# A two-layer attention and mixture-of-experts kernel: three routing batches, expert weights prepared early and kept in DRAM, 8 of 32 shared tiles moved behind the routed ones

## The reference, cut to what matters

```python
x = x + L0_ffn(L0_cond(x))        # attention with 16 heads; relu^2 FFN of 1024, then a 5-step spike count
x = x + L1_ffn(L1_cond(x))        # attention with 16 heads; then the block below

def L1_ffn(X):
    nx = rmsnorm(X, g1)
    X = X + attention4(nx)                          # 4 heads, one shared K and V
    xf = rmsnorm(X, g2)
    rw = softmax(xf @ Wr.T + expert_bias)           # 8 experts
    topw, topi = top_k(rw, 2); topw = softmax(topw)
    shared = swiglu(xf, sW1, sW2, sW3)              # every token
    eo[e] = (silu(xf @ eW1[e].T) * (xf @ eW3[e].T)) @ eW2[e].T
    return X + shared + sum over the 2 chosen e of topw * eo[e]
```

## Time and profile before

| | us |
|---|---|
| runs (3) | 1443.48, 1443.55, 1451.34; median 1443.55 |
| the profiled execution, its own time | 1444.31 |
| its span, first to last instruction | 1442.6 |
| mean granted TensorE clock | 0.962 of full speed |

### The profile page before, as it was taken

One profiled execution on the slowest core, in us unless ns is written; L12 is line 12 of the kernel. 1 busy time (PEld: TensorE's weight loads), 2 busy tenths in 40 slices (PEclk: granted clock), 3 DMA queues, 4 the chain that ended last, 5 costly groups with the idle time before them and its releaser, 6 DMA issues.

```text
span 1442.6 us, 43140 instructions
## 1 busy us (share of the span) xinstructions
PE 1299.9 (90%) x15310; PEld 1147.9 (80%) x15311; DVE 1035.3 (72%) x2129; ACT 896.2 (62%) x2309; POOL 710.8 (49%) x797
## 2 busy tenths in 40 slices
PE   4899999999689999889999999689998689999990
PEld 4799999998579999778888888568877578888870
DVE  4798988888736555787887787778887576555546
ACT  3676777767356666656666676477776254555545
POOL 2556565564435454445445444367766662333330
PEclk9899999999799999999999999899999899999995
DMA  8200000001030000000000000020001623333319
GB/s 230 54 9 10 8 11 8 8 10 38 2 87 1 1 0 1 3 10 10 9 8 10 9 8 13 21 58 15 16 15 63 221 87 116 104 104 101 103 42 349
DMA packets 87021, 71.15 MB, mean 49 GB/s; under 512 B 49981, under 2 KB 80831, under 8 KB 85824
## 3 DMA queue, kind: packets, MB, share of 16 engines
q1 hardware_dynamic: 80320, 51.73, 12.6%
q0 software_dynamic: 6528, 17.05, 3.3%
HBM read 39.47 MB, written 24.02 MB: 44 GB/s over the span
## 4 chain that ended last, share of the span: by engine, by line
PE 53%; issue 21%; POOL 10%; DVE 9%; ACT 4%; another core or an unknown queue 1%; DMA 1%; DVEq 0%; ACTq 0%; POOLq 0%; SPq 0%
PE psQ L2332 8%; PE psQ L1946 7%; PE psW L2024 7%; PE psW L2311 5%; POOL pn L758 5%; PE psQ L2137 3%; POOL rq L784 3%; PE psS L2137 3%; PE psW L2125 3%; PE psM L2125 3%; PE psS L2048 2%; PE psT L1975 2%; PE psT L2059 2%; PE psM L1998 2%; PE psT L2319 2%
## 5 line engine op out<-in xcount | busy, mean ns | idle before, releaser
L1946 PE MATMUL psQ<-xT,wq 128*128 128x256 f32 x1536 | 225.2, 298 | 3.5 <-ACT cur L1114 1.8
L1946 PEld LDWEIGHTS psQ<-xT,wq 128*128 128x128 f32 x1536 | 205.3, 201 | 4.5 <-issue 2.5
L2024 PE MATMUL psW<-wout,oT 128*128 128x256 f32 x1536 | 205.5, 292 | 1.1 <-ACT oT L977 1.1
L2024 PEld LDWEIGHTS psW<-wout,oT 128*128 128x128 f32 x1536 | 194.3, 197 | 1.3 <-ACT oT L977 1.3
L2332 PE MATMUL psQ<-W,exT 128*128 (+1 forms) x624 | 171.2, 410 | 0.0
L758 POOL TENSOR_TENSOR pn<-ex,rden 128x1024 f32<-128x1024 f32 x64 | 124.5, 1945 | 43.5 <-DVE rden L1437 43.5
L977 ACT ACTIVATE oT<-psT,small 128x512 fp32r<-128x512 f32 x128 | 81.1, 685 | 91.3 <-PE psT L2059 91.2
L802 POOL TENSOR_TENSOR hT<-hf,hT 128x512 fp32r<-128x512 f32 x64 | 85.9, 1341 | 102.1 <-ACT hT L1110 101.9
L912 POOL DMA_INDIRECT results<-result,idx x72 | 70.1, 974 | 133.7 <-ACT result L1241 128.7
L770 POOL TENSOR_TENSOR masked_bias<-bias_t,negmask 128x1024 f32<-128x1024 f32 x32 | 68.9, 2152 | 132.5 <-DVE ex L1405 132.5
L1364 DVE SCALAR_TENSOR_TENSOR oT<-psT,small,oT 128x512 fp32r<-128x512 f32 x128 | 90.2, 746 | 55.9 <-ACT oT L977 55.9
(11 more groups left out here) (302 smaller groups left out, 3374.6 us busy)
## 6 DMA issues: line engine op xcount, KB each, us to landing
rows<-sorted SPq DMA_DIRECT2D x72, 132.0 KB, 2.1
both<-results SPq DMA_DIRECT2D x8, 1024.0 KB, 11.8
raw_w<-W SPq DMA_DIRECT2D x27, 256.0 KB, 3.8
vv<-vp SPq DMA_DIRECT2D x256, 16.0 KB, 1.8
out<-X SPq DMA_DIRECT2D x8, 512.0 KB, 8.8
X<-x SPq DMA_DIRECT2D x1, 3584.0 KB, 18.4
bvv<-v_all SPq DMA_DIRECT2D x128, 16.0 KB, 1.8
sorted<-rows SPq DMA_DIRECT2D x9, 132.0 KB
```

Of the source, the lines that this page charges most:

```text
L1946: mm = nc.tensor.matmul(psQ[:, cc, h * QT:h * QT + QT], wq[w][:, k, c * P:c * P + P], xT[g % 2][u][:, k, :], start=(k == 0 and j == 0), st ...
L2024: mm = nc.tensor.matmul(psW[:, 0:D], oT[u][:, c, :], wout[w][:, c, :], start=(u == 0 and c == 0 and w == 0), stop=(u == 1 and c == CH - 1))
```

## The change: what it does

1. **Weights.** A new pass lies in the FFN. SP loads pieces of 256 KB of raw weights into four buffers (two in the place of `xT`, two in `ffn_work`), DVE alone makes hi and lo (`split_piece`), SP writes both (512 KB) to a DRAM array `parked`, waits until that has landed, and only then loads piece n+4. The 27 pieces lie between the FFN groups on DVE, by `PARKED`. `load_expert` becomes one DMA of 1.5 MB per expert from `parked`; the second expert's is issued once the first has landed. `split_expert` goes.
2. **Routing** has three batches of 12, 12 and 8. The first two are ranked inside the block; 14 of the 64 sends lie in block steps 26 to 39, one a step; the later ones are gated by `(t - 7) * 22 // 24 + 1` transposed tiles.
3. **Order.** `FIRST` is 24: 24 shared tiles, 72 routed, 8 shared.
4. **Weights of the tokens** are worked out in shared steps 9 to 21, with ACT's exponentials in steps 18 and 20.
5. **The end.** ACT and DVE do part of the scaling and summing between steps 103 and 107; groups 1, 3 and 5 are added by GpSimd.
6. DVE's and GpSimd's block loops, and DVE's FFN loop, are written out.

```diff
-FIRST = TILES
+FIRST = 3 * TILES // 4
-BATCHES = ((0, 20), (20, TILES))
-FIRST_CHOICE, SECOND_CHOICE, RANK, PLACES = (-6, 5), (-5, 6), (-2, 7), (-1, 8)
-SENT_AHEAD = 3
-ENDS, SLOTS, MARGINS = (10, 12, 14), (16, 18, 20, 22, 24), 26
+BATCHES = ((0, 12), (12, 24), (24, TILES))
+FIRST_CHOICE, SECOND_CHOICE, PLACES = (-14, -2, 5), (-13, -1, 6), (-11, 1, 8)
+RANKED_BEFORE, RANK = (19, 31), 7
+SEND_STEP, SENT_IN_BLOCK = 26, 14
+ENDS, SLOTS, WEIGHTS = (10, 11, 12), (13, 14, 15, 16, 17), (9, 18, 20, 22)
+POOL_GROUPS = (1, 3, 5)
+SCALE_STEP, SUM_STEP = {103: 0, 104: 1, 105: 2, 106: 3, 107: 4}, {104: 0, 106: 2}
+PARKED = [4, 5, 5, 5, 4, 4, 0]
+PIECES = KD + 1
 # SP, behind the loads of layer 1
+            def park(n):
+                p, part = divmod(n, PIECES)
+                sp.wait_ge(sem("p_lo"), n + 1)
+                sp.dma_start(parked[p, :, :, part * 2 * D:part * 2 * D + 2 * D], piece[n % 4][:].bitcast(F32)).then_inc(sem("p_kept"), 16)
+                sp.wait_ge(sem("p_kept"), 16 * (n + 1))
+            for n in range(4):
+                load_piece(n)
+            for n in range(PIECES * EP):
+                park(n)
+                if n + 4 < PIECES * EP:
+                    load_piece(n + 4)
             def load_expert(p, slot, done):
-                w13 = raw_w[:, slot, 1, 0:2 * KD * D].rearrange("p (k w n) -> p k w n", k=KD, w=2)
...
+                sp.dma_start(W[:, slot, :, :].bitcast(F32), parked[p]).then_inc(done, 16)
             sp.wait_ge(sem("t_oev"), 2 * TILES)
-            for p in range(2):
-                load_expert(p, SHARED_SLOT + p, sem("e_first"))
+            load_expert(0, SHARED_SLOT, sem("e_weights"))
+            sp.wait_ge(sem("e_weights"), 16)
+            load_expert(1, SHARED_SLOT + 1, sem("e_weights"))
...
-            for p in (3, EP - 1, EP - 2):
-                load_expert(p, (p + 1) % EP, sem("e_rest"))
-            for p in range(4, EP - 2):
-                load_expert(p, p + 1, sem("e_last"))
+            for p in range(3, EP):
+                load_expert(p, (p + 1) % EP, sem("e_weights"))
 # GpSimd
+                if n >= SENT_IN_BLOCK and k == 0:
+                    pool.wait_ge(sem("e_xTp"), (t - SENT_IN_BLOCK // TOP_K) * 22 // 24 + 1)
+                send(t, k)
...
+            for n, g in enumerate(POOL_GROUPS):
+                x = X[:, G4 * g:G4 * g + G4, :]
+                pool.wait_ge(sem("y_scaled"), g + 1)
+                nc.gpsimd.tensor_tensor(x, x, both[g][:, :, 0, :], ALU.add).then_inc(sem("y_half"), 1)
+                pool.wait_ge(sem("y_half"), 2 * n + 1)
+                nc.gpsimd.tensor_tensor(x, x, both[g][:, :, 1, :], ALU.add).then_inc(sem("y_half"), 1)
 # ACT
             def first_half(i):
-                for piece in range(3 * EP):
-                    if SPLIT_STEP[piece] == i:
-                        split_expert(piece // 3, piece % 3)
+                if i == WEIGHTS[1]:
+                    act.wait_ge(sem("r_exp_in"), 2)
+                    nc.scalar.activation(logits[:], logits[:], ACT.Exp).then_inc(sem("r_exp"), 1)
+                    nc.scalar.activation(top_w[1][:], top_w[1][:], ACT.Exp).then_inc(sem("r_exp"), 1)
+                elif i == WEIGHTS[2]:
+                    act.wait_ge(sem("r_exp_in"), 3)
+                    nc.scalar.activation(weight[1], weight[1], ACT.Exp).then_inc(sem("r_exp"), 1)
...
-                for k in ((0, 1) if g % 2 else (1,)):
+                for k in ((0, 1) if g in POOL_GROUPS else (1,)):
...
+            def other_half(i):
+                if i in SCALE_STEP:
+                    if i == min(SCALE_STEP):
+                        act.wait_ge(sem("r_exp_in"), 4)
+                    scale_results(SCALE_STEP[i])
 # DVE
+            def split_piece(n):
+                part = n % PIECES
+                hi, lo = piece[n % 4][:, 0, :], piece[n % 4][:, 1, :]
+                raw = raw_piece[n % 4][:, 1, :]
+                dve.wait_ge(sem(f"p_raw{n % 4}"), ...)
+                if part < KD:
+                    then(nc.vector.tensor_scalar(hi, raw, g2col[:, part:part + 1], None, ALU.mult))
+                    ins = nc.vector.scalar_tensor_tensor(lo, raw, g2col[:, part:part + 1], hi.bitcast(F32), ALU.mult, ALU.subtract)
+                else:
+                    then(nc.vector.tensor_copy(hi, raw))
+                    ins = nc.vector.tensor_tensor(lo, raw, hi.bitcast(F32), ALU.subtract)
+                ins.then_inc(sem("p_lo"), 1)
...
+            for g in range(GROUPS):
+                ffn(g, g % 2, first=g == 0, last=g == GROUPS - 1)
+                if g < GROUPS - 1:
+                    for n in range(sum(PARKED[:g]), sum(PARKED[:g + 1])):
+                        split_piece(n)
+                if g == 0:
+                    dve.wait_ge(sem("t_oev"), TILES)
```

More of the change, by code:

```diff
@@ L158, in pipeline, with expert_steps @@
             between(i)
-SPLIT_STEP = [-4, -3, -2, 0, 1, 2, 3, 4, 5] + list(range(10, 28))
-def expert_steps(eng, step, first_half=None):
+PARKED = [4, 5, 5, 5, 4, 4, 0]
+PIECES = KD + 1
+assert sum(PARKED) == PIECES * EP
+def expert_steps(eng, step, first_half=None, other_half=None):
     end = FIRST + ROUTED
@@ L505, in rank_columns @@
             n = BATCHES[b][1] - BATCHES[b][0]
[L506 removed]
+            return psM[:, 0:(n + 1) * E] if b == 2 else psW[:, D:D + (n + 1) * E]
         def rank_bank(b):
@@ L676, in _ @@
             for g in range(GROUPS):
-                sp.wait_ge(sem("y_acc"), g + 1)
+                done = sum(h not in POOL_GROUPS for h in range(g + 1))
+                if g in POOL_GROUPS:
+                    sp.wait_ge(sem("y_half"), 2 * (g + 1 - done))
+                else:
+                    sp.wait_ge(sem("y_acc"), done)
                 sp.dma_start(out_dram[:, G4 * g:G4 * g + G4, :], X[:, G4 * g:G4 * g + G4, :]).then_inc(sem("stored"), 16)
@@ L1614, in ffn, with then @@
                             split_q_lo(LAYERS[1], k)
-            ffn_in_lo(0, 0)
-            ffn(0, 0, first=True)
-            dve.wait_ge(sem("t_oev"), TILES)
-            ffn(1, 1)
-            with dve.Fori(1, GROUPS // 2 - 1) as pair:
-                ffn(2 * pair, 0)
-                ffn(2 * pair + 1, 1)
-            ffn(GROUPS - 2, 0)
-            ffn(GROUPS - 1, 1, last=True)
+            chained = 0
+            def then(ins):
+                nonlocal chained
+                chained += 1
+                ins.then_inc(sem("r_chain"), 1)
+                dve.wait_ge(sem("r_chain"), chained)
+            def split_piece(n):
+                part = n % PIECES
+                hi, lo = piece[n % 4][:, 0, :], piece[n % 4][:, 1, :]
+                raw = raw_piece[n % 4][:, 1, :]
+                dve.wait_ge(sem(f"p_raw{n % 4}"), (0 if n % 4 else 16) + sum(16 if m % PIECES == KD else 32 for m in range(n % 4, n + 1, 4)))
+                if part < KD:
+                    then(nc.vector.tensor_scalar(hi, raw, g2col[:, part:part + 1], None, ALU.mult))
+                    ins = nc.vector.scalar_tensor_tensor(lo, raw, g2col[:, part:part + 1], hi.bitcast(F32), ALU.mult, ALU.subtract)
+                else:
+                    then(nc.vector.tensor_copy(hi, raw))
+                    ins = nc.vector.tensor_tensor(lo, raw, hi.bitcast(F32), ALU.subtract)
+                ins.then_inc(sem("p_lo"), 1)
+            ffn_in_lo(0, 0)
+            for g in range(GROUPS):
[5 more added lines that the diff above has]
+                    dve.wait_ge(sem("t_oev"), TILES)
             for t in range(2):
@@ L1791, in _, with read_ranks, places @@
             ends = end_tile[(E.bit_length() - 1) % 2]
-            def places(b):
-                low, high = BATCHES[b]
-                tiles = slice(low, high)
+            def read_ranks(b):
                 dve.wait_ge(sem("r_ranked"), b + 1)
                 ranks, total = rank_bank(b)
-                then(nc.vector.tensor_tensor(place_of[:, tiles, :], ranks, every_tile(next_row[b][:], b), ALU.add))
+                then(nc.vector.tensor_tensor(place_of[:, slice(*BATCHES[b]), :], ranks, every_tile(next_row[b][:], b), ALU.add))
+                nc.vector.tensor_tensor(next_row[b + 1][:], total, next_row[b][:], ALU.add).then_inc(sem("r_read"), 1)
+                dve.wait_ge(sem("r_read"), b + 1)
+            def places(b):
+                tiles = slice(*BATCHES[b])
+                if b == 2:
+                    read_ranks(b)
                 for k in range(TOP_K):
@@ L1886, in first_half @@
                     tile_slots(SLOTS.index(i))
-                elif i == MARGINS:
+                elif i == WEIGHTS[0]:
                     margins()
-                for piece in range(3 * EP):
-                    if SPLIT_STEP[piece] == i:
-                        split_expert(piece // 3, piece % 3)
+                if i == WEIGHTS[2] - 1:
+                    top_weights()
+                elif i == WEIGHTS[3] - 1:
+                    late_weights()
             def merged(i):
```

156 lines of the change are left out of this document (63 added, 93 removed).

## The result

The changed kernel takes 1448.36 us (median of 20 runs) against 1444.8 for the kernel before (20 runs), a ratio of 1.0026, 95% interval 1.0015 to 1.0037. So it is slower, as forecast, but by a quarter of a per cent and not by the 1.2% that the sum gave. It lies at the lower edge of the forecast's own range (1447 to 1477), and inside that of the rival "one of the two large waits is absent" (1436 to 1452). One execution of the kernel under "Slower gates" took 3884 us and is left out.

The account below looks back on a forecast made before the run. PE bounds the FFN; in the block PE and DVE are both close. Terms 18.4 + 4 + 4 - 24.7 + 9 + 3 + 1.5 + 2.6 = +17.8 on 1444.3 give 1462.1, 1461 against the median; range 1426 to 1484.

Parts of the forecast that it names:

- one of the two large waits is absent: Rival: either the FFN burst is hidden or the expert loads stop nobody; about 1443 (1436 to 1452), chance 0.19.
- Pieces in the FFN: FFN: bursts of five weight pieces on DVE delay the statistics, GpSimd and PE, with clock loss behind; +18.4 us.
- Start of the block: Block start: DMAs bringing v queue behind the wait for the first 1.5 MB expert load; +4 us (0.7 to 8).
- Block: Block: added choice, ranks and places +5.2, three lo pieces gone -2.2, fourteen GpSimd sends +1.2; +4 us (0 to 8).
- Shared tiles: Stage before routed tiles: eight tiles leave -24.7, larger loads +9, table loads +3, last sends nearer +1.5; -11.2 us.
- this load costs 12.9 us: Shared tiles, kernel before: loading six experts delays two tiles, 18.0 us less 2 x 2.53.
- the +9: Shared tiles: expert loads of 9.4 instead of 4.7 MB stop engines longer, 21.9 us lost against 12.9.
- the rival of the threefold loss: Shared tiles: loads cost +26 us instead of +9; 1478 (1470 to 1492), chance 0.17.
- The -24.7: Shared tiles: eight tiles leave the path to the first routed tile, saving 24.7 us.
- both absent: Rival: burst hidden and loads stop nobody, GpSimd's 50 sends decide; 1425 (1418 to 1434), chance 0.20.
- Table loads: Shared steps 18 and 20: exponentials bring up to four table loads of 1.28 us between silus; +3 us (0 to 5.1).
- The end: After the last routed tiles: ACT's scales, GpSimd's sums beside ACT and three stores end at +40.0, not 37.4; +2.6 us.

Follow-up runs that it names:

- Slower gates: Changed kernel with sends behind the block gated more slowly, by min((t - 7) * 11 // 10 + 4, 24) transposed tiles: 1.005 of the kernel before.
- the repair: Changed kernel with no burst of five pieces in the FFN, PARKED = [4, 4, 4, 4, 4, 4, 3]: 0.9967 of the kernel before.
- the experiment that takes the wait away: Changed kernel, other send gates, first two expert loads in six of 512 KB behind v transfers, seven later loads in three pieces each: 1.0007 of the kernel before.
- the second trace of the change: Changed kernel unchanged, run again on the same chip as the kernel before: 1.0039 of the kernel before.

## Why the prediction was wrong

By its own steps, with the stretch of the table that each belongs to:

- *Pieces in the FFN*, +18.4 forecast, +12.4 measured in the first trace and 10.4 in the median of nine. The mechanism was right in every link, and the repair confirms it; the term was mis-sized. The gaps are 2.0 to 2.7 us and not 4.7. The clock, taken at +4, cost 5.4 in the first trace and 2.1 to 3.5 where it fell behind one gap only. The store was taken at 3.5 and measured 3.05, the reload 3.5 against 2.7, a piece 1.4 against 1.2. I had leaned on the row of 256 KB at 3.8 us, whose 27 transfers run side by side with others; the `rows<-sorted` row, alone on its queue, was the nearer one. The page now has these transfers at medians of 2.2 and 2.8 us.
- *Start of the block*, +4 forecast, +4.5 measured (387.1 to 391.6). Right, and the experiment that takes the wait away shows that it is this wait.
- *Block*, +4 forecast, -0.7 and +0.3 measured. The added choice, ranks, places and sends are there; the step that the sum left out, at nothing and without a reason, is that two engines' block loops are written out: alone it makes the kernel before some 4 us faster, 1.7 of them in the block if two chips may be compared. The 1.2 us that the sum has for the sends were worked out from no row. Whether the rest is slack no run shows.
- *Shared tiles*, -11.2 forecast, -16.5 and -20.0 measured. This is the step that failed: "this load costs 12.9 us", and from it the +9 and the rival of the threefold loss. The loads cost nothing: with no sends beside them PE was busy 30.00 of 30.00 us, the sign that the prediction had named for this error. The holes come with runs of sends, and stay where they are when the loads move. They don't scale with the bytes; above 2.53 us a tile the stage lost 28.8 us before (32 tiles) and 32.6 after (24 tiles, with the wait for rows and the table loads in it). The -24.7 isn't what the move buys either: the sends set a floor, which I had worked out for the rival "both absent" and left out of the forecast.
- *Table loads*: four are there, 1.28 us each at 1187.76 to 1197.25, with PE gaps of 0.9, 0.2, 0.6 and 0.2 us behind them; about +2 as part of the stage.
- *The end*, +2.6 forecast, +7.3 measured. I had ACT as the bound and GpSimd "beside ACT". DVE is the bound: its first sum comes 13.7 us behind the last routed product, where before it was 8.3, and then GpSimd's sums hold it for 9.0 us. Without them it has three groups more and ends at nearly the same time.

Of the whole, the misses of the FFN (6 to 8), of the block (about 4) and of the shared stage (5 to 9) made the forecast too high, that of the end (about 5) too low. That the sign came out right owes as much to this as to the reasoning: the loss by loads doesn't exist, and a loss by sends, which the forecast didn't have, stood in its place. The Trainium skill (Runtime: NRT & Kernel Launch, section Instruction fetch mechanics), by which the loading of code is mostly hidden, was the better guide here than my row: full DMA engines did not stop an engine, as the 30.00 of 30.00 us shows. The "issue" in the earlier trace rows isn't a wait for code either, since none moved in that hole.

## What to carry to other kernels

A hole that coincides with a load isn't caused by it: before the price of one is put into a sum, look for the same hole elsewhere in the trace (here those that the trace of the kernel before has at 1143 and 1153, with no load beside them) and for what else began just before it. When work moves off the critical path, work out which floor comes next (here 50 sends of 1.28 us) and put it into the forecast itself. A burst in front of something that another in-order engine waits for is free up to that slack and costs in full beyond it: four pieces cost nothing, five cost 2.3 to 5.7 us, of which 2.0 to 2.7 are the wait and the rest is the lower clock behind it.

## What the runs showed of the hardware

- In runs of about six and more indirect sends at 1.28 us each, TensorE's signals reach the other engines late: ACT took up at 1136.62 what PE had transposed at 1127.60, the signal being recorded at 1136.60. GpSimd, waiting for PE too, stopped sending at 1137.3, and the signals that were still due came together, 2.1 us later. The same is seen in the kernel before (sends to 1132.3, signals from 1134.5) and in the second trace of the change (1140.0, 1142.4). Why is open. One chip of the three showed none of it in four kernels, with the same 1.28 us between sends and up to 60 in a row.
- DVE's SCALAR_TENSOR_TENSOR with both inputs in SBUF waits out GpSimd's sum: 2.12 to 2.57 us instead of 0.48. GpSimd's own takes 2.4 to 2.5 us; a sum of the same size took 2.15 in the kernel before; that DVE makes the difference isn't shown. The Trainium skill (SBUF — State Buffer, section SBUF: two separate sides) says that the two share a port pair as an exclusive lock, held for the whole instruction. The trace agrees: each of four instructions in a row ends 0.3 us behind one of GpSimd's. A DVE sum that began at 1425.14, 0.1 us ahead of GpSimd's, took its usual 1.23 us, and GpSimd's then 3.34.
- In the FFN one piece's `lo` (L1661, two inputs in SBUF as well) took 1.67 us instead of 0.69 beside GpSimd's L833 (448.94 to 450.31).
